# Attention stage of a transformer block: two PSUM banks for the output, three for the score maxima, and both output copies on ScalarE

## The chip, the cores and the metric

The kernel runs on one core of a Trainium2 chip. The time is the device time of one execution, in microseconds.

## The reference

One transformer block with conditioning. Here x has B = 2, L = 2048, C = 576; H = 16 heads of D = 36; the hidden layer has 2304 units. All is float32.

```
ada = silu(c) @ W_ada + b_ada                  # shift, scale, gate, twice
h = layernorm(x) * (1 + scale) + shift
q, k, v = split(h @ W_qkv + b_qkv)             # 16 heads of 36
attn = softmax((q * D**-0.5) @ k.T)            # 2048 x 2048 for each of 32 (batch, head)
x = x + gate * ((attn @ v) @ W_proj + b_proj)
x = x + gate2 * (gelu(modulated layernorm(x) @ W_fc1 + b_fc1) @ W_fc2 + b_fc2)
```

## The kernel before

Four stages follow each other: the projection to q, k and v (up to 450 us), attention (450 to 2405 us), the output projection, and the MLP. The change touches only the attention stage, `phase_attention`.

Each of the 32 pairs of batch and head (a "head" below) is worked in two ways at once. For the softmax's maxima, scores with queries on the partitions are computed for one head ahead: `score_max` multiplies a 128-query block with 512 keys into a PSUM bank `sp` (L1029), and VectorE reduces that bank to a maximum per query (L1088). A head has 64 such units. For the softmax itself, scores with keys on the partitions are computed by `scores_t` into a PSUM bank `st` (L1047), with the maxima folded in as two more rows of the operands; ScalarE takes the exponential into `pt` (L1143); `products` multiplies the result with V (37 columns: 36 and one of ones, for the sum) and accumulates in a PSUM bank `op` over eight groups (L1058). The even and the odd key blocks are accumulated apart, on partitions 0 to 36 and 64 to 100 of `op`. Eight groups are a block (512 queries of a head). When it is complete, ScalarE copies the one half to `oa` (L1151), VectorE the other to `ob` (L1121), GpSimd adds them to `oc` (L1207), and SyncE stores `oc` with two DMAs (L994, L995).

PSUM has eight banks; the kernel before gives three to `st`, one to `op` and four to `sp`.

The order is written out ahead in `plan`, a list of 258 steps. On TensorE a step is, in this order: in a late step the transpose of a head's maxima (L1035); then eight pairs of one `score_max` and one `scores_t` matmul; then the products for the exponentials of the step before. A head is eight steps. A block is complete after two steps, and its copies stand at the start of the next odd step (b = 3, 5, ...) on ScalarE and VectorE, ahead of that step's exponentials and reductions. The late step is the last of each head's eight (b = 7, 15, ...) and is odd, too: in it VectorE first splits the transposed maxima in two parts (L1100, L1102), which SyncE writes into `qs` by DMA. `score_max` runs 72 units ahead of `scores_t`, so that the last steps (from b = 247) have no maxima to compute; in five of these (b = 249 to 253) one matmul of the next stage (`turn`, L1066) stands behind the scores.

The waits that matter: a use of an `sp` bank waits until the use four earlier has been read (`slot_free`, in which the bank of use k is `sp[k % 4]`); `scores_t` x waits for exponential x - 3; the first product of a block waits until both copies of the block before are done. Each engine works through its own list in order.

Of the kernel before, what the change touches and what calls it, by code (L numbers as in the profile page):

```python
# [9 lines left out]
ALU = mybir.AluOpType  # L10
# [847 lines left out]
def phase_attention(nc, A, W, ident, qs0, ks0, qs1, ks1, mx, nm, mh, ml, gd, W_proj, b_proj, xf, qkh, qkl, vd, ot,  # L858
# [6 lines left out]

    NB = 3
    NP = 8  # L870
    G = NH * 32
# [11 lines left out]
    ob = [A.sb(f"ob{i}", [VW, 512]) for i in range(2)]  # L883
    oc = W.oc
    st = [A.ps(f"st{i}", [128, 512]) for i in range(3)]
    op = A.ps("op", [128, 512])
    sp = [A.ps(f"sp{i}", [128, 512]) for i in range(4)]
    s_qk, s_m, s_v, s_o = A.sems("qk", NB), A.sems("m", NB), A.sems("v", 2), W.s_o
    s_one = A.sem("one")
    s_s, s_mx, s_nm, s_mt, s_mh = A.sem("s"), A.sem("mx"), A.sem("nm"), A.sem("mt"), A.sem("mh")  # L890
# [8 lines left out]
    for b in range(NBAT + 2):  # L899
        s = Step()  # L900
        s.b, s.last = b, None
        s.late = plan[-1].last if plan else None
        s.slot = None
        if s.late is not None:
            s.slot = len(slots)
            slots.append(("mh", s.late))
        s.units = [[] for _ in range(8)]
        for i in range(min(8, NH * 64 - todo)):
            s.units[i].append((todo, len(slots)))
            slots.append(("mx", todo))  # L910
            todo += 1
            if todo % 64 == 0:
                s.last = todo // 64 - 1
        s.turn = s.turn_slot = None
        if LAST < b <= LAST + KT:
            s.turn, s.turn_slot = b - LAST - 1, len(slots)
            slots.append(("turn", s.turn))
        s.now = b - 1 if 0 < b <= NBAT else None
        s.block = (b - 3) // 2 if b > 2 and b % 2 else None
        plan.append(s)  # L920

    def slot_free(e, k):

        if k > 3:
            kind, n = slots[k - 4]
            if kind == "mx":
                e.wait_ge(s_mx, n - THERE + 1)
            elif kind == "turn":
                e.wait_ge(W.s_u, n + 1)
            else:  # L930
                e.wait_ge(s_mh, 2 * n)
# [91 lines left out]
    def tensor(e):  # L1023
        def score_max(n, slot):
            h, k = divmod(n, 64)
            qb, k4, i = k // 4, k % 4, h % NB
            loaded(e, h)
            slot_free(e, slot)
            e.matmul(sp[slot % 4][:, :], qs[i][0:108, qb * 128:qb * 128 + 128], ks[i][0:108, k4 * 512:k4 * 512 + 512],  # L1029
                     start=True, stop=True).then_inc(s_s, 1)  # L1030

        def max_rows(h, slot):
            e.wait_ge(s_nm, h)
            slot_free(e, slot)
            e.transpose(sp[slot % 4][0:16, 0:128], nm[:, :], ident[:, :]).then_inc(s_mt, 1)  # L1035

        def scores_t(x):
            h, u, kb = x // 64, (x // 16) % 4, x % 16
            i = h % NB
            if x % 64 == 0:  # L1040
                if h == 2:
                    e.wait_ge(s_one, 16)
                loaded(e, h)
                rows_there(e, h)
            if x > 2:
                e.wait_ge(s_p, x - 2)
            e.matmul(st[x % 3][:, :], ks[i][0:110, kb * 128:kb * 128 + 128], qs[i][0:110, u * 512:u * 512 + 512],  # L1047
                     start=True, stop=True).then_inc(s_st, 1)

        def products(g):  # L1050
            h, blk, j = g // 32, g // 8, g % 8
            if g % 32 == 0:
                e.wait_ge(s_v[h % 2], 16 * (h // 2 + 1))
            if j == 0 and blk:
                e.wait_ge(s_oa, 2 * blk)
            e.wait_ge(s_p, 2 * g + 2)
            for a in range(2):
                ins = e.matmul(op[64 * a:64 * a + VW, :], vs[h % 2][:, 2 * j + a, :],  # L1058
                               pt[g % NP][:, a * 512:a * 512 + 512], start=j == 0, stop=j == 7)
            ins.then_inc(s_pv, 1)  # L1060

        def turn(kt, slot):
            e.wait_ge(W.s_sel, 5)
            e.wait_ge(W.s_rr, 32 * HCH)
            slot_free(e, slot)
            e.matmul(sp[slot % 4][:, :], W.sel[:, kt, :], W.rr[:, 0, :], start=True, stop=True).then_inc(W.s_ta, 1)  # L1066

        for s in plan:
            if s.late is not None:
                max_rows(s.late, s.slot)  # L1070
            for q in range(8):
                for n, slot in s.units[q]:
                    score_max(n, slot)
                if s.b < NBAT:
                    scores_t(8 * s.b + q)
            if s.turn is not None:
                turn(s.turn, s.turn_slot)
            if s.now is not None:
                for q in range(4):
                    products(4 * s.now + q)  # L1080

    def vector(e):
        def score_max(n, slot):
            k = n % 64
            e.wait_ge(s_s, n - THERE + 1)
            if k < 2:
                e.wait_ge(s_nm, n // 64 - 1)
            e.tensor_reduce(mx[:, k // 4, k % 4:k % 4 + 1], sp[slot % 4][:, :], AX.X, ALU.max).then_inc(s_mx, 1)  # L1088

        def row_max(h):  # L1090
            e.wait_ge(s_mx, 64 * (h + 1) - THERE)
            if h > 1:
                e.wait_ge(s_mt, h - 1)
            e.tensor_reduce(nm[:, :], mx[:, :, :], AX.X, ALU.max, negate=True).then_inc(s_nm, 1)

        def max_rows(h, slot):
            e.wait_ge(s_mt, h)
            rows_there(e, h - 1)
            src = sp[slot % 4][0:16, 0:128]
            e.tensor_copy(mh[:, :], src).then_inc(s_mh, 1)  # L1100
            e.wait_ge(s_mh, 2 * h - 1)
            e.tensor_tensor(ml[:, :], src, mh[:, :].bitcast(F), ALU.subtract).then_inc(s_mh, 1)  # L1102

        def select():
            e.memset(W.sel[:, :, :].bitcast(F), 0.0).then_inc(W.s_sel, 1)
            e.wait_ge(W.s_sel, 1)
            e.wait_ge(W.s_who, 3)
            cols, who = W.sel[:, :, :].rearrange("h k c -> h (k c)"), W.x1[0:H, 0, :]
            for r in (0, 32):
                e.tensor_copy(cols[r:r + H, 0:C], who).then_inc(W.s_sel, 1)  # L1110
                e.tensor_copy(cols[r:r + H, C:640], who[:, 512:C]).then_inc(W.s_sel, 1)

        for s in plan:
            if s.late is not None:
                max_rows(s.late, s.slot)
            if s.block is not None:
                i = s.block % 2
                e.wait_ge(s_pv, 8 * (s.block + 1))
                if s.block > 1:
                    e.wait_ge(s_oc, s.block - 1)  # L1120
                e.tensor_copy(ob[i][:, :], op[0:VW, :]).then_inc(s_oa, 1)  # L1121
            for q in range(8):
                for n, slot in s.units[q]:
                    score_max(n, slot)
                    if n % 64 == 63:
                        row_max(n // 64)
            if s.block == INV:
                W.invert(e, 0)
            if s.b == LAST:
                select()  # L1130
            if s.turn is not None:
                e.wait_ge(W.s_ta, s.turn + 1)
                e.wait_ge(W.s_a[0], 48)
                e.tensor_tensor(W.oi[:, s.turn, :], sp[s.turn_slot % 4][:, :], W.oi[:, s.turn, :], ALU.mult).then_inc(
                    W.s_u, 1)

    def scalar(e):
        def exps(x):
            g, a = divmod(x, 2)
            e.wait_ge(s_st, x + 1)  # L1140
            if g >= NP and a == 0:
                e.wait_ge(s_pv, g - NP + 1)
            e.activation(pt[g % NP][:, a * 512:a * 512 + 512], st[x % 3][:, :], ACT.Exp, scale=SCALE).then_inc(s_p, 1)  # L1143

        for s in plan:
            if s.block is not None:
                i = s.block % 2
                e.wait_ge(s_pv, 8 * (s.block + 1))
                if s.block > 1:
                    e.wait_ge(s_oc, s.block - 1)  # L1150
                e.activation(oa[i][:, :], op[64:64 + VW, :], ACT.Copy).then_inc(s_oa, 1)  # L1151
            if s.b < NBAT:
                for q in range(8):
                    exps(8 * s.b + q)
            if s.block == INV + 1:
                W.high(e, 0)
            i, kt = weight(s.b - 2)
            if i is not None:
                W.w[i].high(e, kt, W.stg)
            if s.turn is not None:  # L1160
                e.wait_ge(W.s_u, s.turn + 1)
                e.activation(W.ah[:, s.turn, :], W.oi[:, s.turn, :], ACT.Copy).then_inc(W.s_ah, 1)
# [697 lines left out]
```

## Time and profile before

| | |
|---|---|
| median of 3 runs | 3534.35 us (3531.66 to 3534.86) |
| the profiled execution | 3534.86 us; its span, from the first to the last instruction, 3532.8 us |
| mean granted TensorE clock | 0.991 |
| TensorE busy | 3466.9 us, 98% of the span |
| VectorE, ScalarE, GpSimd busy | 1960.5, 1495.6, 363.4 us |

The busy time of TensorE counts from a matmul's start to its modelled end; matmuls overlap, so the start of the next one says more than the length of one. PEld is the load of weights ahead of a matmul.

### The profile page before, as it was taken

What the parts mean: (1) busy time and instruction counts of PE and PEld (TensorE: products, weight loads), DVE (VectorE), ACT (ScalarE), POOL (GpSimd) and SP (SyncE); (2) the same over time, 40 slices, a digit from 0 to 9 for tenths busy, and PEclk for the clock granted to TensorE, in tenths of its full rate; (3) what the DMA queues carried; (4) which work ended last, traced back from release to release, by engine and by line L of the source; (5) the groups of instructions that cost most, each with busy time, mean ns of one, the idle gap of its engine ahead of it and who ended that gap; (6) DMA issues with size and microseconds to landing.
All of it is one profiled execution on the core that took longest, in us unless ns stands there. A gap on an engine that the chain in (4) does not pass through costs nothing. (4 is left out here: it accounts for less than half of the span.)

```text
span 3532.8 us, 46449 instructions
## 1 busy us (share of the span) xinstructions
PE 3466.9 (98%) x16991; PEld 2289.0 (65%) x16991; DVE 1960.5 (55%) x3544; ACT 1495.6 (42%) x2776; POOL 363.4 (10%) x284
## 2 busy tenths in 40 slices
PE   8999999999999999999999999999889999999999
PEld 6888854454544444445445454436778989898988
DVE  5446566666766666677676676635553232433232
ACT  3223255565555555555555555554541110201010
POOL 1000010111100000010000000024511010000000
PEclk9999999999999999999999999999899999999999
DMA  6453421212111121212111111115753222422221
GB/s 207 161 169 141 144 80 30 64 40 59 37 41 42 30 52 30 55 30 53 32 48 35 35 48 29 33 34 172 258 186 99 68 94 68 157 76 88 74 88 51
DMA packets 144661, 285.54 MB, mean 81 GB/s; under 512 B 18276, under 2 KB 44132, under 8 KB 137524
## 3 DMA queue, kind: packets, MB, share of 16 engines
q1 hardware_dynamic: 144440, 282.57, 26.1%
q8 instruction: 142, 2.33, 0.3%
q14 instruction: 79, 0.65, 0.1%
HBM read 177.09 MB, written 104.34 MB: 80 GB/s over the span
## 5 line engine op out<-in xcount | busy, mean ns | idle before, releaser
L1088 DVE TENSOR_REDUCE q_mx<-b_sp 128x1 f32<-128x512 f32 x1976 | 1202.4, 677 | 307.7 <-PE b_sp L1029 307.6
L1143 ACT ACTIVATE b_pt<-b_st 128x512 f32<-128x512 f32 x2048 | 1043.9, 624 | 464.5 <-PE b_st L1047 452.9
L1058 PE MATMUL b_op<-b_pt,b_vs 128*37 128x512 f32 x4096 | 934.3, 598 | 0.0
L1058 PEld LDWEIGHTS b_op<-b_pt,b_vs 128*37 128x37 f32 x4096 | 224.5, 114 | 571.5 <-issue 447.4
L1815 ACT ACTIVATE d_af<-n_pf,q_mx 128x512 f32<-128x512 f32 x144 | 99.0, 687 | 731.2 <-PE n_pf L1738 730.4
L1755 PE MATMUL d_pm<-d_vl,d_ah 128*128 128x288 f32 x1152 | 339.4, 295 | 0.0
L1756 PE MATMUL d_pm<-d_vh,d_al 128*128 128x288 f32 x1152 | 339.3, 295 | 0.0
L1754 PE MATMUL d_pm<-d_vh,d_ah 128*128 128x288 f32 x1152 | 339.2, 294 | 0.0
L1207 POOL TENSOR_TENSOR w_oc<-b_oa,b_ob 37x512 f32<-37x512 f32 x128 | 164.6, 1286 | 1634.7 <-DVE b_ob L1121 1624.2
L1029 PE MATMUL b_sp<-q_hh,q_lo 108*128 108x512 f32 x696 | 290.1, 417 | 5.7 <-PEq L850 4.5
L1047 PE MATMUL b_st<-q_lo,q_hh 110*128 110x512 f32 x704 | 281.2, 404 | 2.6 <-ACT b_pt L1143 2.6
L1047 PE MATMUL b_st<-q_qs,q_ks 110*128 110x512 f32 x704 | 280.0, 398 | 0.4 <-ACT b_pt L1143 0.4
L1029 PE MATMUL b_sp<-b_ks,b_qs 108*128 108x512 f32 x640 | 265.4, 415 | 1.2 <-DVE q_mx L1088 0.3
L1029 PE MATMUL b_sp<-q_ks,q_qs 108*128 108x512 f32 x640 | 265.6, 415 | 0.9
L1047 PE MATMUL b_st<-b_qs,b_ks 110*128 110x512 f32 x640 | 253.2, 396 | 0.0
L1151 ACT ACTIVATE b_oa<-b_op 37x512 f32<-37x512 f32 x128 | 76.1, 595 | 357.5 <-PE b_op L1058 357.5
L1121 DVE COPY b_ob<-b_op 37x512 f32<-37x512 f32 x128 | 87.0, 680 | 241.1 <-PE b_op L1058 241.0
L1776 DVE CAST d_ah<-d_af 128x512 fp32r<-128x512 f32 x144 | 61.5, 427 | 281.4 <-ACT d_af L1815 281.4
L1754 PEld LDWEIGHTS d_pm<-d_vh,d_ah 128*128 128x128 f32 x1152 | 216.2, 188 | 0.7
L1755 PEld LDWEIGHTS d_pm<-d_vl,d_ah 128*128 128x128 f32 x1152 | 216.1, 188 | 0.7
L1756 PEld LDWEIGHTS d_pm<-d_vh,d_al 128*128 128x128 f32 x1152 | 216.2, 188 | 0.0
L1029 PEld LDWEIGHTS b_sp<-q_hh,q_lo 108*128 108x128 f32 x696 | 132.4, 190 | 114.0 <-issue 88.6
(300 smaller groups left out, 4635.8 us busy)
## 6 DMA issues: line engine op xcount, KB each, us to landing
qkh<-a_th SPq DMA_DIRECT2D x72, 256.0 KB, 2.0
qkl<-a_tl SPq DMA_DIRECT2D x72, 256.0 KB, 2.1
d_yi<-y SPq DMA_DIRECT2D x64, 288.0 KB, 3.0
vd<-a_vx SPq DMA_DIRECT2D x8, 1184.0 KB, 6.2
b_vs<-vd SPq DMA_DIRECT2D x32, 296.0 KB, 2.9
a_x<-in_x SPq DMA_DIRECT2D x8, 1152.0 KB, 6.3
ot<-w_oc SPq DMA_DIRECT2D x128, 72.0 KB
y<-d_yi SPq DMA_DIRECT2D x32, 288.0 KB, 2.2
```

Source lines behind the costliest of these rows:

```text
L1029: e.matmul(sp[slot % 4][:, :], qs[i][0:108, qb * 128:qb * 128 + 128], ks[i][0:108, k4 * 512:k4 * 512 + 512], start=True, stop=True).then_i ...
L1047: e.matmul(st[x % 3][:, :], ks[i][0:110, kb * 128:kb * 128 + 128], qs[i][0:110, u * 512:u * 512 + 512], start=True, stop=True).then_inc(s_ ...
L1058: ins = e.matmul(op[64 * a:64 * a + VW, :], vs[h % 2][:, 2 * j + a, :], pt[g % NP][:, a * 512:a * 512 + 512], start=j == 0, stop=j == 7)
L1088: e.tensor_reduce(mx[:, k // 4, k % 4:k % 4 + 1], sp[slot % 4][:, :], AX.X, ALU.max).then_inc(s_mx, 1)
L1121: e.tensor_copy(ob[i][:, :], op[0:VW, :]).then_inc(s_oa, 1)
L1143: e.activation(pt[g % NP][:, a * 512:a * 512 + 512], st[x % 3][:, :], ACT.Exp, scale=SCALE).then_inc(s_p, 1)
L1151: e.activation(oa[i][:, :], op[64:64 + VW, :], ACT.Copy).then_inc(s_oa, 1)
L1207: e.tensor_tensor(oc[i][:, :], oa[i][:, :], ob[i][:, :], ALU.add).then_inc(s_oc, 1)
L1754: e.matmul(out, ah[:, f, ts], vh[:, f, cs], start=f == 0, stop=False)
L1755: e.matmul(out, ah[:, f, ts], vl[:, f, cs], start=False, stop=False)
L1756: ins = e.matmul(out, al[:, f, ts], vh[:, f, cs], start=False, stop=f == NT - 1)
L1815: e.activation(af[m % 2][:, :], pf[m % 4][:, :], ACT.Gelu_apprx_tanh, bias=b1[:, half * NT + f:half * NT + f + 1]).then_inc(s_af, 1)
```

## The change

`op` gets a second bank, and blocks alternate between the two; `sp` gives one up and has three. In the order of TensorE the third to the eighth `score_max` of a step move behind the `scores_t` matmul that they preceded: m0 s0 m1 s1 s2 m2 s3 m3 s4 m4 s5 m5 s6 m6 s7 m7 in place of m0 s0 m1 s1 m2 s2 ... m7 s7. Both copies of a block are made by ScalarE, one after the other, behind the step's exponentials; VectorE makes none. A use of `sp` waits for the use three earlier, and the first product of a block for the copies of the block before last. The diff, without the places where `slot % 4` becomes `slot % 3`:

```diff
     st = [A.ps(f"st{i}", [128, 512]) for i in range(3)]
-    op = A.ps("op", [128, 512])
-    sp = [A.ps(f"sp{i}", [128, 512]) for i in range(4)]
+    op = [A.ps(f"op{i}", [128, 512]) for i in range(2)]
+    sp = [A.ps(f"sp{i}", [128, 512]) for i in range(3)]
...
-        s.units = [[] for _ in range(8)]
+        s.units = [[] for _ in range(9)]
         for i in range(min(8, NH * 64 - todo)):
-            s.units[i].append((todo, len(slots)))
+            s.units[(0, 1, 3, 4, 5, 6, 7, 8)[i]].append((todo, len(slots)))
...
     def slot_free(e, k):
 
-        if k > 3:
-            kind, n = slots[k - 4]
+        if k > 2:
+            kind, n = slots[k - 3]
...
         def products(g):
...
-            if j == 0 and blk:
-                e.wait_ge(s_oa, 2 * blk)
+            if j == 0 and blk > 1:
+                e.wait_ge(s_oa, 2 * (blk - 1))
             e.wait_ge(s_p, 2 * g + 2)
             for a in range(2):
-                ins = e.matmul(op[64 * a:64 * a + VW, :], vs[h % 2][:, 2 * j + a, :],
+                ins = e.matmul(op[blk % 2][64 * a:64 * a + VW, :], vs[h % 2][:, 2 * j + a, :],
                                pt[g % NP][:, a * 512:a * 512 + 512], start=j == 0, stop=j == 7)
...
         for s in plan:
             if s.late is not None:
                 max_rows(s.late, s.slot)
-            for q in range(8):
+            for q in range(9):
                 for n, slot in s.units[q]:
                     score_max(n, slot)
-                if s.b < NBAT:
+                if q < 8 and s.b < NBAT:
                     scores_t(8 * s.b + q)
...
     def vector(e):
...
-            if s.block is not None:
-                i = s.block % 2
-                e.wait_ge(s_pv, 8 * (s.block + 1))
-                if s.block > 1:
-                    e.wait_ge(s_oc, s.block - 1)
-                e.tensor_copy(ob[i][:, :], op[0:VW, :]).then_inc(s_oa, 1)
-            for q in range(8):
+            for q in range(9):
...
     def scalar(e):
...
         for s in plan:
+            if s.b < NBAT:
+                for q in range(8):
+                    exps(8 * s.b + q)
             if s.block is not None:
                 i = s.block % 2
                 e.wait_ge(s_pv, 8 * (s.block + 1))
                 if s.block > 1:
                     e.wait_ge(s_oc, s.block - 1)
-                e.activation(oa[i][:, :], op[64:64 + VW, :], ACT.Copy).then_inc(s_oa, 1)
-            if s.b < NBAT:
-                for q in range(8):
-                    exps(8 * s.b + q)
+                e.activation(oa[i][:, :], op[i][64:64 + VW, :], ACT.Copy).then_inc(s_oa, 1)
+                e.activation(ob[i][:, :], op[i][0:VW, :], ACT.Copy).then_inc(s_oa, 1)
```

## Rows read from the trace of the kernel before

**Rows 1.** The page: the span, and TensorE's busy time, share and instructions.
```profile
span 3532.8 us, 46449 instructions
PE 3466.9 (98%) x16991; PEld 2289.0 (65%) x16991; DVE 1960.5 (55%) x3544; ACT 1495.6 (42%) x2776; POOL 363.4 (10%) x284
```

**Rows 2.** Stretches of the attention stage: length, busy time per engine, granted clock, DMA share.
```profile
500.00:2320.00 1820.00, 1816.71 (x7687) 898.96 (x7683) 1260.00 (x2122) 1052.42 (x2043) 183.61 (x141) 1.00 0.16 42
```

**Rows 3.** The page's groups of instructions: the two copies out of op.
```profile
L1151 ACT ACTIVATE b_oa<-b_op 37x512 f32<-37x512 f32 x128 | 76.1, 595 | 357.5 <-PE b_op L1058 357.5
L1121 DVE COPY b_ob<-b_op 37x512 f32<-37x512 f32 x128 | 87.0, 680 | 241.1 <-PE b_op L1058 241.0
```

**Rows 4.** One group of instructions by tile: the transposes of the late steps.
```profile
L1035 PE MATMUL b_sp<-g_ident,q_nm x31: 277/277/278, 501.3 to 2327.4; 128*16 128x128 f32 x31
```

**Rows 5.** Timeline, an even step: start, length, instruction [idle before it <- releaser].
```profile
1513.54 0.19 PEld L1029 LDWEIGHTS b_sp<-q_ks,q_qs 108*128 108x128 f32 x1 [0.83 <-issue]
...
1513.88 0.40 PE L1047 MATMUL b_st<-b_qs,b_ks 110*128 110x512 f32 x1
...
1514.08 4.88 DVE L1088 TENSOR_REDUCE q_mx<-b_sp 128x1 f32<-128x512 f32 x8 [2.48 <-PE b_sp L1029]
...
1514.31 4.03 ACT L1143 ACTIVATE b_pt<-b_st 128x512 f32<-128x512 f32 x8 [3.50 <-PE b_st L1047]
...
1515.76 1.11 ACT L1143 ACTIVATE b_pt<-b_st 128x512 f32<-128x512 f32 x2
...
1516.48 0.68 DVE L1088 TENSOR_REDUCE q_mx<-b_sp 128x1 f32<-128x512 f32 x1
...
1516.92 0.39 PE L1029 MATMUL b_sp<-q_ks,q_qs 108*128 108x512 f32 x1
...
1517.15 0.40 PE L1047 MATMUL b_st<-b_qs,b_ks 110*128 110x512 f32 x1
...
1517.48 0.12 PEld L1058 LDWEIGHTS b_op<-b_pt,b_vs 128*37 128x37 f32 x2 [0.37 <-ACT b_pt L1143]
...
1521.04 0.19 PEld L1029 LDWEIGHTS b_sp<-q_ks,q_qs 108*128 108x128 f32 x1 [0.83 <-issue]
```

**Rows 6.** Timeline, the odd step before it, same columns.
```profile
1506.02 0.19 PEld L1029 LDWEIGHTS b_sp<-q_ks,q_qs 108*128 108x128 f32 x1 [0.83 <-issue]
...
1506.14 0.68 DVE L1121 COPY b_ob<-b_op 37x512 f32<-37x512 f32 x1 [2.21 <-PE b_op L1058]
...
1507.94 1.27 DVE L1088 TENSOR_REDUCE q_mx<-b_sp 128x1 f32<-128x512 f32 x2
...
1509.33 0.19 PEld L1029 LDWEIGHTS b_sp<-q_ks,q_qs 108*128 108x128 f32 x1 [0.20 <-issue]
...
1509.98 0.12 PEld L1058 LDWEIGHTS b_op<-b_pt,b_vs 128*37 128x37 f32 x2 [0.36 <-issue]
```

**Rows 7.** Timeline, a late step (the 17th of 31), same columns.
```profile
1475.23 0.09 PEld L1035 LDWEIGHTS b_sp<-g_ident,q_nm 128*16 128x16 f32 x1 [0.83 <-issue]
...
1475.86 0.28 DVE L1102 TENSOR_TENSOR q_ml<-b_sp,q_mh 16x128 fp32r<-16x128 f32 x1
...
1476.07 0.67 DVE L1121 COPY b_ob<-b_op 37x512 f32<-37x512 f32 x1
...
1477.27 0.67 DVE L1088 TENSOR_REDUCE q_mx<-b_sp 128x1 f32<-128x512 f32 x1
...
1478.05 0.19 PEld L1029 LDWEIGHTS b_sp<-q_ks,q_qs 108*128 108x128 f32 x1 [0.30 <-issue]
...
1479.25 0.19 PEld L1029 LDWEIGHTS b_sp<-q_ks,q_qs 108*128 108x128 f32 x1 [0.30 <-issue]
...
1479.92 0.12 PEld L1058 LDWEIGHTS b_op<-b_pt,b_vs 128*37 128x37 f32 x2 [0.37 <-issue]
```

**Rows 8.** Stretches of the last steps, columns as in rows 2.
```profile
2341.90:2351.30 9.40, 8.98 (x27) 2.73 (x25) 1.38 (x2) 5.25 (x10) 2.17 (x2) 0.82 0.41 134
2351.30:2358.90 7.60, 7.38 (x28) 2.48 (x26) 0.69 (x1) 4.66 (x9) 1.75 (x2) 1.00 0.00 0
```

More of the change, by code:

```diff
@@ L1028, in score_max @@
             slot_free(e, slot)
-            e.matmul(sp[slot % 4][:, :], qs[i][0:108, qb * 128:qb * 128 + 128], ks[i][0:108, k4 * 512:k4 * 512 + 512],
+            e.matmul(sp[slot % 3][:, :], qs[i][0:108, qb * 128:qb * 128 + 128], ks[i][0:108, k4 * 512:k4 * 512 + 512],
                      start=True, stop=True).then_inc(s_s, 1)
@@ L1034, in max_rows @@
             slot_free(e, slot)
-            e.transpose(sp[slot % 4][0:16, 0:128], nm[:, :], ident[:, :]).then_inc(s_mt, 1)
+            e.transpose(sp[slot % 3][0:16, 0:128], nm[:, :], ident[:, :]).then_inc(s_mt, 1)
         def scores_t(x):
@@ L1065, in turn @@
             slot_free(e, slot)
-            e.matmul(sp[slot % 4][:, :], W.sel[:, kt, :], W.rr[:, 0, :], start=True, stop=True).then_inc(W.s_ta, 1)
+            e.matmul(sp[slot % 3][:, :], W.sel[:, kt, :], W.rr[:, 0, :], start=True, stop=True).then_inc(W.s_ta, 1)
         for s in plan:
@@ L1087, in score_max @@
                 e.wait_ge(s_nm, n // 64 - 1)
-            e.tensor_reduce(mx[:, k // 4, k % 4:k % 4 + 1], sp[slot % 4][:, :], AX.X, ALU.max).then_inc(s_mx, 1)
+            e.tensor_reduce(mx[:, k // 4, k % 4:k % 4 + 1], sp[slot % 3][:, :], AX.X, ALU.max).then_inc(s_mx, 1)
         def row_max(h):
@@ L1098, in max_rows @@
             rows_there(e, h - 1)
-            src = sp[slot % 4][0:16, 0:128]
+            src = sp[slot % 3][0:16, 0:128]
             e.tensor_copy(mh[:, :], src).then_inc(s_mh, 1)
@@ L1133, in vector @@
                 e.wait_ge(W.s_a[0], 48)
-                e.tensor_tensor(W.oi[:, s.turn, :], sp[s.turn_slot % 4][:, :], W.oi[:, s.turn, :], ALU.mult).then_inc(
+                e.tensor_tensor(W.oi[:, s.turn, :], sp[s.turn_slot % 3][:, :], W.oi[:, s.turn, :], ALU.mult).then_inc(
                     W.s_u, 1)
```

## The prediction

> **What bounds the kernel now.** The page comes first: TensorE is busy for 98% of the span, VectorE for 55%, ScalarE for 42% [rows 1]. In the attention stage, which is what the change touches, TensorE is busy for 1816.71 of 1820.00 us at a granted clock of 1.00, VectorE for 1260 and ScalarE for 1052 [rows 2]. So the stage is a chain of matmuls, and the question for each edit is whether it makes TensorE's next weight load late. A busy share can't answer that; the timeline of single steps does.
>
> Three kinds of step occur. All times below are from the step's first weight load, and m0 to m7, s0 to s7, r0 to r7 and e0 to e7 are its score matmuls for the maximum, its transposed score matmuls, the reductions and the exponentials. In an even step [rows 5] the 16 score matmuls follow each other every 0.23 us; s7, the last, starts at 3.61 and the first product p at 3.94; the products take the rest, and the next step begins at 7.50. VectorE starts r0 at 0.54 and ends r7 at 5.42, so its pace is (4.88 - 0.68) / 7 = 0.60 us. ScalarE starts e0 at 0.77 and has done all eight at 4.80. TensorE issues a pair (m, s) every 0.47 us: inside the score part it runs ahead of VectorE by 0.13 us a pair, and the sp buffers are what lets it. Over the whole step VectorE has 2.1 us to spare, but a bank is needed at its own moment.
>
> In an odd step [rows 6] VectorE first copies op (0.68 us), r3 ends at 1507.94 + 1.27 = 1509.21, and the weight load of m7, which waits for r3, starts at 1509.33 after 0.20 us idle: 0.12 us from the end of a reduction to the load that it releases. The step loses hardly anything: p starts at 3.96.
>
> In a late step [rows 7] VectorE also handles the transposed maxima. There TensorE does wait: m5's load starts at 1478.05, 0.11 us after r1's end (1477.27 + 0.67), m7's at 1479.25, and p only at 4.69, so the step takes 4.69 - 3.94 = 0.75 us more than an even one. The 31 transposes stand (2327.4 - 501.3) / 30 = 60.87 us apart [rows 4]; that is one head of eight steps: four even ones of 7.50, one late one of 8.25, which leaves 7.54 for each of three odd ones, whose p is thus at 3.98 on average.
>
> **The change, part by part.** *Second bank for op: nothing gained.* In before, both copies of a block start 0.1 us into the odd step and take 0.68 and 0.59 us [rows 3, 6]; the bank is wanted again by p at 3.96. No weight load of a product waits for a copy. The Trainium skill's page Perfetto Trace Analysis (Optimizing Tensor Performance, Matmuls) would have independent matmul groups rotate through different PSUM banks so that the evacuation of one overlaps the next group; by it, the second bank should pay. The trace has the copy already under 3.2 us of other matmuls, so by the row it pays 0; the same rule, read for sp, speaks against taking the bank there.
>
> *Both copies on ScalarE, behind the exponentials.* ScalarE ends e7 at 4.80; two copies of 0.595 [rows 3] bring it to 6.0, and its next exponential is wanted at 7.50 + 0.77 = 8.27. Cover 2.3 us, cost 0. In a late step the exponentials can end up to 0.75 us later, as the step is that much longer; still covered. GpSimd's addition and SyncE's two stores of the block come about 5 us later in the step; behind them on SyncE's queue are loads for a head that is needed seven or more steps of 7.5 us later. In the new order the bank must be free two blocks on, a whole step after the copies: cost 0. VectorE loses 0.68 us in every odd step, which by itself is 0.04 us of p there (3.98 to 3.94).
>
> *Three sp banks instead of four, m2 to m7 behind their s.* Now m7 waits for r4, not r3. The moved order gives it half a pair: it would start at 3.61 instead of 3.38, s7 at 3.38. r4 starts at 1516.48 and ends at 3.62 [rows 5], and nothing in the new order starts it later: m4, tenth of the 16, starts at about 0.1 + 9 x 0.234 = 2.2 and is done by 2.7, and r4 starts at 2.94 at VectorE's own pace. From its end: 0.11 us to m7's load; from that load to p, in the late step, 0.67 us with s7 between (1479.25 to 1479.92), so 0.67 - 0.23 = 0.44 without. Hence p at 3.62 + 0.11 + 0.44 = 4.17 in even and odd steps alike: +0.23 on 3.94, +0.19 on 3.98. m6, which waits for r3 (3.02), is late by 0.1, inside this; m5 and before are free. On the other side s7 moves forward and waits for e4, which ends at 1515.76 + 1.11 = 3.33; s7 can then start some 0.1 us late, and m7 after it at 3.71, before r4 allows it. So that wait lies under the other.
>
> *Late steps gain.* The copy is gone from VectorE, so r0 starts where it stood (1476.07, 0.84) and r4 ends at 0.84 + 4 x 0.60 + 0.67 = 3.91; p at 3.91 + 0.11 + 0.44 = 4.46 against 4.69: -0.23. One reduction more is waited for, one copy less, and s7 no longer stands behind m7.
>
> *The last steps gain.* Without maxima to compute, TensorE is held by the exponentials. In the three odd ones with a turn (2341.90, 2358.90, 2375.90) ScalarE's copy delays e0, and each takes 9.40 us at a granted clock of 0.82; the even ones between take 7.6 at 1.00 [rows 8]. With the copy behind the exponentials an odd one should look like an even one: 3 x (9.4 - 7.6) = -5.4, if the clock stays up. Two further odd steps save about 0.2 each, and the final block's two copies in series instead of side by side (2 x 0.595 against 0.68) give 0.5 back: together 0.
>
> *Unknown cost and its ends.* No row shows m7's late load directly ahead of a product. What is open is how much of a late load's 0.19 us shows. The matmul behind a late load is followed 0.34 us after the load, not 0.23 (1513.54 to 1513.88) [rows 5], so 0.10 of it shows, and this is in the 0.44. If none showed, p would be at 4.07; if all did, at 4.26. I take 0.10, since the late step agrees: its 0.67 from m7's load to p is this 0.34 and the 0.33 from s7 to p in the even step.
>
> *Sum.* A head changes by 4 x 0.23 + 3 x 0.19 - 0.23 = +1.26 us; 30 heads +37.8; the seven steps ahead of the first late one +1.5; the last steps -5.4: +33.9. The profiled execution took 3534.86 us (span 3532.8 and 2.1 around it), the slowest of the three, 0.5 over their median. 3534.86 + 33.9 - 0.5 = **3568 us**.
>
> **The rivals.** *Third bank is enough (faster).* If r4's end didn't hold m7, only the gains would stand: 0.04 x 92 odd steps = 4, 30 late steps x 0.23 = 7, the last steps 5.4: 3518 us. For it: VectorE has 2.1 us free per step. It decides where r4 ends before 3.62 - 0.23 + 0.13 - 0.11 = 3.41, for a load may be some 0.13 late unseen (the odd step's, at 3.31, is 0.16 behind its turn at 3.15, and p loses 0.02 to 0.04); that is a pace of (3.41 - 0.54 - 0.68) / 4 = 0.55 us. Even and odd steps show 0.60. Chance 5%.
>
> *Losses and gains near each other.* None of a late load shows: 4 x 0.13 + 3 x 0.09 - 0.33 = +0.46 a head, +15 in all, less 5.4: 3544; with a little less it is within the 0.2% (7 us) which is about what a measurement of this kernel can tell from no change. Chance 6% for the latter.
>
> *The two waits add.* If e4's hold on s7 came on top of r4's on m7, 0.1 us more in 217 steps: 3590. Against it: m7's load depends on r4's end, which s7 doesn't move. Chance 8%.
>
> *The clock falls in the main steps.* With a gap in every step TensorE could be granted half its clock for a while, as in rows 8, where one fall costs 1.8 us. Once a head: 30 x 1.8 = 54 more, 3622. Against it: a late step already has an idle of 0.30 us ahead of each of several loads [rows 7], and the stage's clock is 1.00 over 30 of them [rows 2]. The Trainium skill's page TensorE: Matmul & The Clock Gate (A second HAM failure mode) describes TensorE idling briefly between groups as it cycles through PSUM banks, and the clock going up and down with it; by that rule this rival is what the change brings, and the trace agrees only in the last steps. Chance 3%.
>
> **How the numbers follow.** The forecast has 78%, slower by 34 us. With the other two slow rivals that makes 89% slower, 6% within 0.2%, 5% faster. All of a late load showing gives 4 x 0.32 + 3 x 0.28 - 0.14 = 1.98 a head, +62 in all: 3596 without the gain of the last steps. Halfway from the forecast to both ends: 3552 to 3588.
>
> **What the profile after would show.** Even and odd steps of equal length, near 7.73; a late step near 8.02; transposes 62.1 us apart. Idle ahead of m7's load in nearly every step, ended by a reduction, with r4's end 0.11 before the load. VectorE's copy gone (87 us less), ScalarE 76 us busier, with both copies starting about 4.8 into odd steps. The last odd steps at 7.6 with a clock of 1.00. I am wrong if r4 ends clearly before 3.6, if p follows m7's load in less than 0.3 us, or if ScalarE's copies push the next exponentials.

## The result

The changed kernel takes 3573.47 us (median of 4 runs, 3565.8 to 3576.6) against 3533.01 us before: a ratio of 1.0111 (95% interval 1.0095 to 1.0127), 40 us slower. The forecast was 3568 us, slower by 34, in a range of 3552 to 3588. A second series (below) gave 3571.56 us and the same ratio.

The page after, its first lines, answers to [rows 1]:

```profile
span 3574.4 us, 46322 instructions
...
PE 3511.3 (98%) x16991; PEld 2255.0 (63%) x16991; DVE 1882.6 (53%) x3416; ACT 1558.3 (44%) x2904; POOL 360.7 (10%) x284
```

VectorE is 78 us less busy and ScalarE 63 us more; forecast were 87 and 76. The copies themselves did what was forecast (the 87.0 us of `ob` on VectorE are gone, 75.7 came to ScalarE); the rest is in other instructions, such as the exponentials, which are 13 us less busy in all (1043.9 before, 1031.0 after), and wasn't followed up. TensorE still shows 98%, and in the attention stage all of it, where [rows 2] had 1816.71 of 1820.00 us. Stretch, busy time of each engine, granted clock, DMA share:

```profile
500.00:2360.00 1860.00, 1860.00 (x7701) 864.03 (x7701) 1190.81 (x2007) 1112.21 (x2167) 180.36 (x141) 1.00 0.16 40
```

A reader who went by busy time would see a stage that got better. The delays are shorter than the overlap of two matmuls, so they don't appear as idle time of PE at all. Nor does a total of the weight loads' waits measure them. The row that is new among the waits is that of `scores_t` for the exponentials (total, times, longest; the first line is the changed kernel, the second the one with the new order alone, for which see below):

```profile
PEld b_st L1046 <- ACT b_pt L1136: 157.6, 864, 0.2
...
PEld b_st L1047 <- ACT b_pt L1143: 215.9, 1122, 0.9
```

The second has more of it and loses only 12 us. What tells is the start of single loads: over the trace, the load of m7 starts at 3.15 us of an even step and 3.31 of an odd one before, and at 3.73 in both after, always 0.11 to 0.12 us behind the end of r4.

The transposes of the late steps give the length of a head, as in [rows 4]:

```profile
L1034 PE MATMUL b_sp<-g_ident,q_nm x31: 276/277/278, 504.6 to 2367.4; 128*16 128x128 f32 x31
```

(2367.4 - 504.6) / 30 = 62.09 us, 1.22 more than the 60.87 before; forecast were 1.26 and 62.1.

An even step, from its first weight load (compare [rows 5]; same columns):

```profile
1505.96 0.19 PEld L1028 LDWEIGHTS b_sp<-q_ks,q_qs 108*128 108x128 f32 x1 [0.83 <-issue]
...
1506.49 4.88 DVE L1087 TENSOR_REDUCE q_mx<-b_sp 128x1 f32<-128x512 f32 x8 [2.85 <-PE b_sp L1028]
...
1507.87 0.19 PEld L1046 LDWEIGHTS b_st<-b_qs,b_ks 110*128 110x128 f32 x1 [0.19 <-ACT b_pt L1136]
...
1508.89 0.68 DVE L1087 TENSOR_REDUCE q_mx<-b_sp 128x1 f32<-128x512 f32 x1
...
1509.69 0.19 PEld L1028 LDWEIGHTS b_sp<-q_ks,q_qs 108*128 108x128 f32 x1 [0.17 <-issue]
...
1510.12 3.63 PE L1057 MATMUL b_op<-b_pt,b_vs 128*37 128x512 f32 x16
1513.68 0.19 PEld L1028 LDWEIGHTS b_sp<-q_ks,q_qs 108*128 108x128 f32 x1 [0.83 <-issue]
```

VectorE's eight reductions last 4.88 us, as before, and start at 0.53. The third row is s4's load, which like those of s3, s5 and s6 waits 0.16 to 0.19 us for an exponential, mostly inside its head start (the time by which a load can be late without making its matmul late). The fourth is r4, which ends at 2.93 + 0.68 = 3.61. m7's load starts at 3.73, 0.12 behind r4's end, after 0.17 us idle. The products start at 4.16 (forecast 4.17), 0.43 behind that load (0.44), and the step takes 7.72. Odd steps have the same length: the trace's steps have medians of 7.73 for both.

A late step (compare [rows 7]):

```profile
1497.94 0.09 PEld L1034 LDWEIGHTS b_sp<-g_ident,q_nm 128*16 128x16 f32 x1 [0.83 <-issue]
...
1498.79 4.85 DVE L1087 TENSOR_REDUCE q_mx<-b_sp 128x1 f32<-128x512 f32 x8
...
1501.96 0.19 PEld L1028 LDWEIGHTS b_sp<-q_ks,q_qs 108*128 108x128 f32 x1 [0.30 <-issue]
...
1502.40 3.63 PE L1057 MATMUL b_op<-b_pt,b_vs 128*37 128x512 f32 x16
1502.77 0.59 ACT L1147 ACTIVATE b_oa<-b_op 37x512 f32<-37x512 f32 x1
1503.39 0.59 ACT L1148 ACTIVATE b_ob<-b_op 37x512 f32<-37x512 f32 x1
...
1505.34 0.30 SPq L993 DMA_DIRECT2D ot<-w_oc  x1
...
1505.96 0.19 PEld L1028 LDWEIGHTS b_sp<-q_ks,q_qs 108*128 108x128 f32 x1 [0.83 <-issue]
```

The reductions start at 0.85, where VectorE's copy stood; p is at 4.46 (forecast 4.46), the step takes 8.02, 0.2 less than before. Both copies stand behind the exponentials and are over at 6.04, under the products.

In the last steps a fall of the clock is left, in an even step (compare [rows 8]; the rows are an odd step, an even one, the even one with the fall, an odd one):

```profile
2381.70:2389.20 7.50, 7.28 (x27) 2.44 (x25) 0.69 (x1) 5.73 (x11) 1.27 (x1) 1.00 0.00 1
2389.20:2396.80 7.60, 7.38 (x28) 2.49 (x26) 0.69 (x1) 4.66 (x9) 1.86 (x2) 1.00 0.50 165
...
2404.30:2413.60 9.30, 9.08 (x27) 2.78 (x25) 0.69 (x1) 4.65 (x9) 4.87 (x4) 0.82 0.03 10
2413.60:2421.20 7.60, 7.38 (x28) 2.51 (x26) 0.69 (x1) 5.73 (x11) 1.73 (x2) 1.00 0.00 0
```

Attention, from its first score matmul to its last product, went from 1952.6 us (450.1 to 2402.7) to 1985.9 (452.5 to 2438.4): +33.3. The span went up by 41.6. The other 8.3 us lie outside: 2.4 ahead of the stage, 5.9 behind it, mostly at the start of the projection; 0.5 of them are the two copies in series at the end, as forecast (from the last product to the first projection matmul 5.0 us against 4.5). The 2.4 us ahead were not there when the kernel was run again (the stage then began at 450.1, as before). Two stretches of before's trace from its first projection matmul:

```profile
2407.10:2411.00 3.90, 3.80 (x15) 3.45 (x15) 0.26 (x1) 0.00 (x0) 0.00 (x0) 0.56 0.72 226
2411.00:2415.00 4.00, 4.00 (x26) 3.45 (x26) 1.25 (x4) 0.33 (x1) 0.00 (x0) 1.00 1.06 304
```

and the same after:

```profile
2443.20:2447.10 3.90, 3.74 (x15) 3.49 (x15) 0.00 (x1) 0.00 (x0) 0.00 (x0) 0.50 0.70 210
2447.10:2451.10 4.00, 4.00 (x15) 3.55 (x15) 1.15 (x2) 0.56 (x1) 0.00 (x0) 0.50 1.07 307
2451.10:2456.10 5.00, 5.00 (x18) 3.95 (x16) 1.40 (x3) 0.70 (x2) 2.56 (x2) 0.50 1.06 333
```

TensorE works at its lower level (1.2 GHz) for some 4 us in the one and 13 in the other, and gets 15 matmuls done in 4 us instead of 26.

### The profile page after: what moved, and what is told of

It is laid out like the page before. It is cut to its first block and busy times, and to the rows that moved or that the text cites. A ratio compares the mean times of both kernels' runs of the same rounds, so it can differ in the third digit from the quotient of the medians.

```text
span 3574.4 us, 46322 instructions
## 1 busy us (share of the span) xinstructions
PE 3511.3 (98%) x16991; PEld 2255.0 (63%) x16991; DVE 1882.6 (53%) x3416; ACT 1558.3 (44%) x2904; POOL 360.7 (10%) x284
## 5 line engine op out<-in xcount | busy, mean ns | idle before, releaser
L1136 ACT ACTIVATE b_pt<-b_st 128x512 f32<-128x512 f32 x2048 | 1031.0, 624 | 783.2 <-PE b_st L1046 783.0
L1046 PE MATMUL b_st<-q_qs,q_ks 110*128 110x512 f32 x704 | 272.5, 408 | 0.2 <-ACT b_pt L1136 0.2
L1783 DVE TENSOR_TENSOR d_ug<-d_pm,d_gt 128x288 f32<-128x288 f32 x128 | 58.5, 457 | 253.5 <-PE d_pm L1750 253.5
L1046 PEld LDWEIGHTS b_st<-q_lo,q_hh 110*128 110x128 f32 x704 | 131.6, 188 | 86.5 <-ACT b_pt L1136 67.8
```

## The experiments

Step lengths below are medians over the trace; the row of the transposes gives a head's length, last minus first by 30.

**The changed kernel again** (no edit).

> The changed kernel once more. Its profile had the attention stage 33 to 36 us longer, and some 8 us more outside it, where no line of the kernel differs (the projection stage began at a granted clock of 0.50 for 13 us where before it was 4 us). My theory: what lies outside isn't the change's; another run has steps of 7.73 (even, odd) and 8.00 us (late) again, to 0.02, while the stages outside can be 0 to 8 us longer than before's. Rival: the longer idle time at the end of attention (two ScalarE copies in series) brings the projection's slow start every time; then it is there again, 5 us long.

3571.56 us (3569.73 to 3574.98, 4 runs) against 3533.18 (15 runs, 3526.56 to 3535.43); ratio 1.0111 (1.0097 to 1.0125). Steps 7.73, 7.73, 8.00. The projection was again at 0.50 for its first 10 us, and what follows attention took 1136.0 us as in the first trace, against 1130.1 before. That alone fits the rival; the later runs speak to it.

**The new order alone**, on the kernel before.

```diff
-        s.units = [[] for _ in range(8)]
+        s.units = [[] for _ in range(9)]
...
-            s.units[i].append((todo, len(slots)))
+            s.units[(0, 1, 3, 4, 5, 6, 7, 8)[i]].append((todo, len(slots)))
```

> The kernel before with one part of the change, the new order of the matmuls; four sp banks, one op bank, copies as before. Theory (m7 waits for a reduction, s7 for e4): with four banks m7 waits for r3 and is free, but s7 stands 0.23 us earlier and waits for e4, which ends at 3.33: s7 at 3.48, m7 at 3.71, p at 4.04, so even and odd steps take 7.60, a late one 8.01: 124 x 0.10 + 92 x 0.06 - 30 x 0.24 = about +11 us, 3544. Rival (only the reductions hold TensorE): even and odd 7.50, late 8.01: -11 us, 3522.

3545.11 us (3542.62 to 3547.34), ratio 1.0035 (1.0023 to 1.0048). Steps 7.61, 7.61, 8.00.

```profile
L1035 PE MATMUL b_sp<-g_ident,q_nm x31: 277/277/278, 502.9 to 2341.9; 128*16 128x128 f32 x31
```

A head takes 61.30. In an odd step that began at 1468.36 (timeline):

```profile
1471.74 0.19 PEld L1047 LDWEIGHTS b_st<-q_lo,q_hh 110*128 110x128 f32 x1 [0.19 <-ACT b_pt L1143]
1471.82 0.42 PE L1047 MATMUL b_st<-q_lo,q_hh 110*128 110x512 f32 x1
1471.85 0.19 PEld L1029 LDWEIGHTS b_sp<-b_ks,b_qs 108*128 108x128 f32 x1
1472.08 0.40 PE L1029 MATMUL b_sp<-b_ks,b_qs 108*128 108x512 f32 x1
1472.40 0.15 PEld L1058 LDWEIGHTS b_op<-b_pt,b_vs 128*37 128x37 f32 x4 [0.37 <-issue]
```

s7's load waits for an exponential, m7's for nothing, and p is at 4.04. The rival is out: the order alone costs 12 us, by ScalarE, because each s from s2 on stands 0.23 us earlier in the order while its bank comes free no earlier. In the kernel before, s7's load at 3.38 is already only 0.06 us behind e4's end.

**The old order in the changed kernel.**

```diff
-            s.units[(0, 1, 3, 4, 5, 6, 7, 8)[i]].append((todo, len(slots)))
+            s.units[i].append((todo, len(slots)))
```

> The changed kernel with the order of the matmuls put back (m7 ahead of s7), three sp banks kept. Theory: r4's end (3.62) holds m7's load at 3.73 as in the changed kernel, and s7 now stands behind it: p at 3.62 + 0.12 + 0.67 = 4.40, steps of 7.96, late ones 8.26: about 57 us more than the changed kernel, some 3625. Rival (the order, not the bank, is what costs; s7's wait for e4 is the hold): without the new order steps go back towards 7.50 to 7.60, and the time falls below the changed kernel's, 3545 or less.

3628.39 us (3625.11 to 3631.96), ratio 1.0271 (1.0257 to 1.0285). Steps 7.96, 7.96, 8.24; a head of 63.95:

```profile
L1034 PE MATMUL b_sp<-g_ident,q_nm x31: 276/277/278, 503.8 to 2422.2; 128*16 128x128 f32 x31
```

The order more than halves the loss: with the old order the changed kernel loses 95 us on before, with the new one 40.

**Shorter reductions in the changed kernel**: 448 of 512 columns, so that the last 64 keys of each 512 are left out of the maxima.

```diff
-            e.tensor_reduce(mx[:, k // 4, k % 4:k % 4 + 1], sp[slot % 3][:, :], AX.X, ALU.max).then_inc(s_mx, 1)
+            e.tensor_reduce(mx[:, k // 4, k % 4:k % 4 + 1], sp[slot % 3][:, 0:448], AX.X, ALU.max).then_inc(s_mx, 1)
```

> The changed kernel with each reduction over 448 of the 512 columns: the last 64 keys of each block of 512 are left out of the maxima. Theory: VectorE's pace falls from 0.60 to 0.53, r4 ends at 3.28 and m7 is free of it; what is left is e4's hold on s7, p at 4.04: steps of 7.60, late ones near 7.69, in all about -4 us on before, 3529. Rival A (e4 holds nothing): 7.50, late 7.60, 3505. Rival B (the reductions' pace isn't the cause): 7.73 stays, 3570.

3533.32 us (10 runs, 3527.52 to 3537.84), ratio 1.0002 (0.9993 to 1.0012). Steps 7.60, 7.60, 7.67. The end of the score part in the odd step that began at 1451.82:

```profile
1454.07 2.73 DVE L1087 TENSOR_REDUCE q_mx<-b_sp 128x1 f32<-128x448 f32 x5
...
1455.20 0.19 PEld L1046 LDWEIGHTS b_st<-q_lo,q_hh 110*128 110x128 f32 x1 [0.19 <-ACT b_pt L1136]
1455.27 0.43 PE L1046 MATMUL b_st<-q_lo,q_hh 110*128 110x512 f32 x1
1455.33 0.19 PEld L1028 LDWEIGHTS b_sp<-b_ks,b_qs 108*128 108x128 f32 x1
1455.54 0.39 PE L1028 MATMUL b_sp<-b_ks,b_qs 108*128 108x512 f32 x1
1455.86 0.15 PEld L1057 LDWEIGHTS b_op<-b_pt,b_vs 128*37 128x37 f32 x4 [0.33 <-ACT b_pt L1136]
```

The idle time ahead of m7's load is gone, the one ahead of s7's stays, and p is at 4.04 again. One step of the theory was off: r4 ends at 3.40, not 3.28, for with shorter reductions VectorE catches up with TensorE's matmuls and runs at a pace of 0.56 us, not 0.53 (0.53 it is in the late step, where its reductions start 0.30 us later). So m7's load (3.51) is still 0.12 behind r4's end, but only 0.03 later than in the run with the new order alone (3.49), and that costs p nothing. 0.07 us less on each of 1976 instructions of an engine with a busy share of 53% takes 38 us off the kernel. Rivals A and B are out.

**The copies at the start of the step again**, oa on ScalarE and ob on VectorE; three sp banks, two op banks, the new order.

```diff
     def vector(e):
...
+            if s.block is not None:
+                i = s.block % 2
+                e.wait_ge(s_pv, 8 * (s.block + 1))
+                if s.block > 0:
+                    e.wait_ge(s_oc, s.block)
+                e.tensor_copy(ob[i][:, :], op[i][0:VW, :]).then_inc(s_oa, 1)
             for q in range(9):
```

> The changed kernel with the copies put back to the start of the odd step, ob on VectorE and oa on ScalarE; three sp banks, two op banks and the new order stay. Theory: in an odd step VectorE starts 0.20 us later, r4 ends at 3.80, p at 4.35: 7.92; in a late step r4 ends at 4.50, p at 5.05: 8.60; even steps stay at 7.73. About 92 x 0.19 + 30 x 0.60 = 35 us more than the changed kernel, plus 4 in the last steps: some 3610. Rival (where the copy stands doesn't matter, since VectorE is idle for over 2 us of each step): as the changed kernel, 3570.

3608.82 us (3603.46 to 3613.7), ratio 1.0218 (1.0204 to 1.0232). Steps 7.73 (even), 7.90 (odd), 8.60 (late). In the odd step that began at 1499.16:

```profile
1499.28 0.68 DVE L1120 COPY b_ob<-b_op 37x512 f32<-37x512 f32 x1 [2.44 <-PE b_op L1057]
...
1503.07 0.19 PEld L1028 LDWEIGHTS b_sp<-b_ks,b_qs 108*128 108x128 f32 x1 [0.30 <-issue]
1503.50 0.63 PE L1057 MATMUL b_op<-b_pt,b_vs 128*37 128x512 f32 x2
```

p at 4.34. So moving the copies behind the exponentials on ScalarE saves 37 us with three banks. VectorE's start is costly with four banks too: there, moving its copy off the start is worth 22 us (below). In this run the copies also wait for GpSimd's addition of the block before, and not of the one before that; in its trace no copy waits for GpSimd.

**The same with one op bank** (`op` a single bank, the first product of a block waiting for the copies of the block before).

> The kernel of the run before with one op bank in place of two (seven banks in use). Theory (the second bank for op is worth nothing): same steps to 0.01 us, same time within 0.2%. Rival (it lets the products start earlier): odd steps longer by up to the copy's 0.68 us, up to 80 us more.

3606.71 us (3604.26 to 3609.36), ratio 1.0213 (1.0199 to 1.0227); steps 7.73, 7.90, 8.60. The second op bank is worth nothing where the copies stand early.

This run differs from the one with the new order alone in the number of `sp` banks and in nothing else. Steps go from 7.61, 7.61 and 8.00 to 7.73, 7.90 and 8.60, the time from 3545 to 3607 (two series; before took 3533.18 and 3532.79 in them): the fourth bank alone was worth 62 us. The 40 us of the whole change are thus, to the 2 us by which series differ, +12 for the order, +62 for the bank, nothing for the second op bank and -37 for the late copies.

**The changed kernel with one op bank**, the copies late.

```diff
-    op = [A.ps(f"op{i}", [128, 512]) for i in range(2)]
+    op = A.ps("op", [128, 512])
...
-            if j == 0 and blk > 1:
-                e.wait_ge(s_oa, 2 * (blk - 1))
+            if j == 0 and blk:
+                e.wait_ge(s_oa, 2 * blk)
```

> The changed kernel with one op bank in place of two; both copies stay on ScalarE behind the exponentials. Theory (the second bank is worth nothing by itself, but is what lets the copies stand so late): the first product of the next block waits for the second copy, which ends at about 5.9, so p at 6.03 in place of 4.17 in every odd step: odd steps 9.6, late ones 9.8, even ones 7.73; about 92 x 1.86 + 30 x 1.75 + 7 = 230 us more than the changed kernel, 3800. Rival (the copies are so far under other work that the bank doesn't matter here either): 3570.

3853.26 us in the single run (before 3532.96). The odd step that began at 1410.12:

```profile
1415.55 0.59 ACT L1148 ACTIVATE b_ob<-b_op 37x512 f32<-37x512 f32 x1
1416.19 0.15 PEld L1057 LDWEIGHTS b_op<-b_pt,b_vs 128*37 128x37 f32 x4 [2.16 <-ACT b_ob L1148]
```

p at 6.07 (6.03 expected), the step 9.64. The mechanism is the expected one, but the time is 53 us over the expected. Most of that is the clock: of the 122 odd steps that have copies and compute maxima, 23 took 11.3 us, one every 6 to 14 steps, which is 23 x 1.7 = 39 us, and the four odd ones behind them took 10.9 to 12.4. TensorE's idle time ahead of p is 1.84 to 1.92 us in the odd steps; in the 30 late ones among the 122 it is 1.57 to 1.59, and none of them had a fall (stretches: the stage, such a step, and the one quoted):

```profile
500.00:2600.00 2100.00, 1888.11 (x7627) 871.35 (x7625) 1182.68 (x1995) 1103.81 (x2152) 177.79 (x139) 0.98 0.14 36
1391.05:1402.39 11.34, 9.49 (x34) 3.93 (x33) 4.87 (x8) 5.21 (x10) 1.27 (x1) 0.85 0.03 8
1410.12:1419.76 9.64, 7.80 (x35) 3.60 (x33) 4.87 (x8) 5.21 (x10) 1.26 (x1) 1.00 0.03 8
```

**The kernel before with VectorE's copy behind the fourth reduction.**

```diff
-            if s.block is not None:
...
-                e.tensor_copy(ob[i][:, :], op[0:VW, :]).then_inc(s_oa, 1)
             for q in range(8):
+                if q == 4 and s.block is not None:
...
+                    e.tensor_copy(ob[i][:, :], op[0:VW, :]).then_inc(s_oa, 1)
```

> The kernel before with one edit: VectorE's copy of op stands behind the step's fourth reduction. Theory: m7 waits for r3, which the copy no longer delays; odd steps 7.50, and a late step has r3 ending at 3.31 and the copy at 3.92, so p at about 4.09 and the step at 7.65 in place of 8.25: -4 and -18 us, 3511. Rival (the copy now ends too late for the products of the next block, whose bank it frees): p waits in all odd steps, no gain or a loss.

3510.41 us (3508.37 to 3517.94) against 3532.79; ratio 0.9941 (0.9928 to 0.9955): 22 us faster than before. Steps 7.50, 7.50, 7.64. A late step that began at 1463.43:

```profile
1464.26 2.46 DVE L1088 TENSOR_REDUCE q_mx<-b_sp 128x1 f32<-128x512 f32 x4
...
1466.65 0.67 DVE L1122 COPY b_ob<-b_op 37x512 f32<-37x512 f32 x1
...
1466.84 0.19 PEld L1029 LDWEIGHTS b_sp<-q_ks,q_qs 108*128 108x128 f32 x1 [0.29 <-issue]
...
1467.51 3.63 PE L1058 MATMUL b_op<-b_pt,b_vs 128*37 128x512 f32 x16
```

r3 ends at 3.29, m7's load is at 3.41, the copy over at 3.89, p at 4.08 (4.09 expected).

**The same, and in the last odd steps both halves copied by VectorE.**

> The kernel of the run before, and in the last odd steps, which compute no maxima, VectorE copies both halves of op, so that ScalarE starts with its exponentials. Theory: those three steps of 9.4 us at a clock of 0.82 become 7.6 at 1.00: 5 us less than the run before, 3506. Rival (the clock's falls there have another cause): the three stay at 9.4.

3511.75 us (3508.65 to 3518.18), ratio 0.9946 (0.9933 to 0.9958): no difference from the run before. In the trace the three steps took 7.57 at a clock of 1.00, as expected, and attention 1926.0 us instead of 1932.5. But the run before hadn't its slow steps where the theory puts them: of its last steps, 9.03 (odd), 9.22 and 9.26 (both even) had the fall, while the three odd ones with a turn took 7.76. So this pair of runs doesn't decide between theory and rival.

## Why the prediction was right

**The sum.** In the attention stage the forecast was +33.9 us and the trace has +33.3: 36.6 for the 30 heads (37.8 forecast), 0.9 ahead of the first late step (1.5), -4.3 behind the last (-5.4). The range doesn't follow from its own rule: halfway from 3568 to the two ends that are worked out, 3544 and 3596, is 3556 to 3582, not 3552 to 3588. The time lies in both.

**TensorE's order and the wait for r4** held to 0.01 us: r4's end at 3.61, 0.12 to the load, 0.43 to p. The open cost, how much of a late load shows, was 0.10, the value taken. Shorter reductions remove the loss, and the old order enlarges it by the 0.23 us that s7 then adds (7.73 to 7.96).

**The wait for e4 lies under the other**: right, and shown by its coming out when the other is taken away (7.60 to 7.61 in two runs). It was priced at nothing rightly, but the first rival forgot it: had r4 not held m7, e4 would still have made the even and the odd steps 7.60, 0.10 more in each of 216, and the time some 3540 us, not 3518 (an estimate; the run with short reductions, whose late steps are 0.33 us shorter besides, took 3533). A speed-up was thus less within reach than the rival said.

**The copies on ScalarE**: both are over at 6.0 of a step, and the exponentials behind them wait for `st` alone. VectorE's gain in the late step was 8.25 - 8.00 = 0.25 (0.23 forecast).

**The second op bank** is worth nothing by itself, and is what permits copies that end at 6 us. The trace of before had said so: a bank that is read within 0.8 us and wanted again at 3.96. The Trainium skill's page Perfetto Trace Analysis (Optimizing Tensor Performance, Matmuls) asks for rotation so that the copy of one group overlaps the next group's matmuls; the runs agree where that overlap is needed (3853 to 3571 us with late copies) and show 3607 against 3609 where other matmuls already cover it.

**The last steps** were right by accident. Their term (-5.4) came out as -4, but that the copy's delay of e0 brings the falls didn't hold: an early copy costs 0.20 us there (7.76 against 7.56, no fall, in the run with the new order alone), and the falls come in odd and in even steps. There were 3, 0, 1, 2 and 3 in the traces with early copies, 1, 1, 1 and 0 in those with late ones on ScalarE, none in the last kernel. Whether the small gaps there make them likelier stays open.

**Outside attention** the forecast had nothing but the 0.5 us of the copies in series, and the traces after have 8 us. The slow start of the projection (0.50 for over 10 us) isn't peculiar to the change: it is in the traces of the changed kernel (twice), of the old order, of the copies at the start and of the kernel before with the copy moved, with serial and with parallel copies at the end; it is absent in those of before, of the order alone, of one op bank with early copies, of the last kernel, and, with the changed kernel's serial copies, of the short reductions and of one op bank with late copies. That refutes the rival that the serial copies bring it every time. What goes with it in the traces is the moment of the fall: in the five with the slow start the clock fell 0.7 to 0.9 us ahead of the first projection matmul and stayed low for 13.7 us; in five of the others it fell 0.2 to 1.4 us behind it and stayed low for 3.4, and in the last kernel it fell 2.4 us ahead and was low for 6.8. The 50th matmul then stands 14.2 us behind the first, or 10.0 (10.5 in the last kernel). What sets the moment, and whether the change makes the long one more frequent, stays open, so these us of the 40 are neither forecast nor explained. Executions of one kernel differ by 5 to 10 us here, of which this may be a part.

**The clock in the main steps** stayed at 1.00, so that rival fell for this change. Gaps of 1.84 us, in the changed kernel with one op bank, do bring it: it was the right mechanism for larger gaps (23 of the 92 odd steps with them, apart from the late ones). The Trainium skill's page TensorE: Matmul & The Clock Gate (A second HAM failure mode) describes such going up and down between groups; the traces agree for gaps of 1.84 us and not for those of 0.2 us.

## What to carry to other kernels

A buffer between a fast bursty producer and a steady consumer is sized by the burst, not by the consumer's share of the time: VectorE was idle for over 2 us of each step, and one bank less still cost 62 us, of which a better place for the copies gave 37 back. Work out for the last use in a burst when its bank is released (start, pace, number of uses ahead) and compare with when it is wanted; where there is 0.1 us of room, order and placement count as much as banks. Moving a filler behind the reductions that are waited for was worth 22 us with the banks as they were.

## What the runs showed of the hardware

From the end of the instruction that frees a bank to the weight load that waits for it: 0.12 us for a reduction, 0.05 for an exponential (with e4 ending at 3.33, s7's load at 3.38). Behind a load that comes too late, the next matmul starts 0.34 us after the load and not 0.23, so 0.10 us of the load's 0.19 show. With waits of 1.84 to 1.92 us in every other step, the granted clock fell in 23 of 92 steps and cost 1.7 us each time; with 1.57 to 1.59 in none of 30.
